# Row scatters of the first expert layer, paced differently in a one-core attention loop on Trainium2

## What is computed

```python
x = x + attn(layernorm(x))      # scores of 8 heads of width 2, leaky relu (0.2), softmax, values
x = x + ffn0(layernorm(x))      # sigmoid gates, top 6 of 64 experts, silu(x@g)*(x@u)@d, plus a shared expert
x = x + lookup(layernorm(x))    # offsets and softmax weights pick from row 0, then one projection
x = x + ffn1(layernorm(x))      # softmax gates, top 2 of 8 experts

def attn_core(q, k, v):
    scores = einsum('bmhd,bnhd->bhmn', q, k) / sqrt(dqk)
    scores = where(scores >= 0, scores, 0.2 * scores)
    return einsum('bhmn,bnhd->bmhd', softmax(scores), v)
```

## Time and profile before

| what | value |
|---|---|
| three runs | 866.82, 868.16, 869.16 us |
| median | 868.16 us |
| profiled execution: its time from the first to the last instruction (span) | 1023.1 us |
| PE busy in the profiled execution | 740.8 us, 72% |
| DVE busy | 604.7 us, 59% |
| ACT busy | 498.4 us, 49% |
| POOL busy | 425.6 us, 42% |
| mean granted TensorE clock | 0.849 of full speed |

### The profile page before, as it was taken

How to read it: one execution, slowest core, us unless ns; L and a number is a source line. 1 busy time by engine, 2 the same in 40 slices (tenths; PEclk the granted TensorE clock), 3 DMA queues, 4 the chain that set the end, 5 groups by cost and what they waited for, 6 DMA issues and landing times.

```text
span 1023.1 us, 18229 instructions
## 1 busy us (share of the span) xinstructions
PE 740.8 (72%) x6306; PEld 444.5 (43%) x6309; DVE 604.7 (59%) x1330; ACT 498.4 (49%) x747; POOL 425.6 (42%) x659
## 2 busy tenths in 40 slices
PE   5799999899889777338899960300377677599992
PEld 3322222222223222138899930200245543399992
DVE  5899998898889755446676410000265766244442
ACT  4788888778777645213444421000344432165550
POOL 4310023522442345366677667776002033345553
PEclk9999999999999878659999995655675776699997
DMA  8999999999992000528866522222000010133346
GB/s 254 249 286 288 283 273 280 288 276 291 310 358 105 19 25 31 129 87 245 258 191 171 157 54 52 54 52 51 0 11 14 19 33 32 37 37 49 48 51 138
DMA packets 83482, 142.96 MB, mean 140 GB/s; under 512 B 10736, under 2 KB 75728, under 8 KB 81888
## 3 DMA queue, kind: packets, MB, share of 16 engines
q1 hardware_dynamic: 57744, 118.07, 40.4%
q0 software_dynamic: 12784, 17.40, 7.8%
q10 hardware_dynamic: 12864, 6.33, 2.3%
HBM read 116.57 MB, written 101.34 MB: 213 GB/s over the span
## 4 chain that ended last, share of the span: by engine, by line
PE 53%; another core or an unknown queue 14%; DVE 9%; ACT 9%; issue 6%; DMA 5%; SPq 2%; POOL 1%; DVEq 0%; POOLq 0%; ACTq 0%
PE PS L664 11%; PE PS L650 8%; PE PS L1010 6%; PE PS L639 6%; DMA XP<-slots_scratch 3%; ACT PB L1146 3%; PE PS L1020 3%; PE PS L802 3%; PE PS L789 2%; PE PS L791 2%; ACT PB L1149 2%; PE PS L777 2%; PE PS L849 1%; ACT PS L1141 1%
## 5 line engine op out<-in xcount | busy, mean ns | idle before, releaser
L1679 DVE TENSOR_SCALAR PS<-PS 128x1024 f32<-128x1024 f32 x241 | 288.1, 1229 | 55.4 <-PE PS L639 30.1
L1146 ACT ACTIVATE PB<-PS 128x1024 f32<-128x1024 f32 x192 | 194.5, 1025 | 52.6 <-PE PS L650 46.0
L664 PE MATMUL PS<-PB,VS 128*32 128x256 f32 x2048 | 168.5, 402 | 3.4 <-issue 3.3
L639 PE MATMUL PS<-QS,KP 64*128 64x512 bf16 (+1 forms) x640 | 101.2, 347 | 38.1 <-ACT PB L1149 18.7
L1393 POOL DMA_INDIRECT slots_scratch<-XN,slot x96 | 93.3, 972 | 61.1 <-ACT PB L1146 36.5
L1453 POOL DMA_INDIRECT GB<-y_scratch,slotc x96 | 90.9, 946 | 37.1 <-issue 29.4
L650 PE MATMUL PS<-QM,KP 64*128 64x512 bf16 (+1 forms) x640 | 102.3, 350 | 3.5 <-DVE PS L1679 3.4
L838 PE MATMUL PS<-wshd,OH 96*128 96x128 f32 x64 | 11.7, 356 | 111.6 <-DVE OH L1820 110.7
L1463 POOL DMA_INDIRECT slots_scratch<-XN,slot x32 | 32.0, 1000 | 140.8 <-DVE slot L1964 130.8
L1483 POOL DMA_INDIRECT sums_scratch<-YO,XG x39 | 60.6, 1555 | 60.9 <-DVE YO L2034 59.7
L1149 ACT ACTIVATE PB<-PS 128x1024 f32<-128x1024 f32 x64 | 64.7, 1026 | 40.5 <-PE PS L650 26.8
(11 more groups left out here) (297 smaller groups left out, 1411.5 us busy)
## 6 DMA issues: line engine op xcount, KB each, us to landing
y_scratch<-YP SPq DMA_DIRECT2D x80, 128.0 KB, 2.5
slots_scratch<-slots_scratch SPq DMA_DIRECT2D x1, 8768.0 KB
W0GU<-in_w0gu SPq DMA_DIRECT2D x1, 6144.0 KB, 50.1
XP<-slots_scratch ACTq DMA_DIRECT2D x80, 64.0 KB, 2.8
XP<-slots_scratch SPq DMA_DIRECT2D x80, 64.0 KB, 2.7
W1GU<-in_w1gu SPq DMA_DIRECT2D x8, 512.0 KB, 4.1
W0D<-in_w0d SPq DMA_DIRECT2D x1, 3072.0 KB
XG<-slots_scratch SPq DMA_DIRECT2D x39, 68.5 KB
```

What stands on the lines that cost most here:

```text
L639: last = mm(o, keys, QS[g][r, x], start=first, stop=True, skip_group_check=not first)
L664: last = mm(PS[32 * j:32 * j + 32, at:at + HALF], VS[:, n, g * HG + j, :], PB[u // 2 % 3][:, 2 * (j % 2) + j // 2, q], start=(n == 0 and h ...
L1146: A(PB[u // 2 % 3][:, 2 * hp:2 * hp + 2, :], pair_banks(u).rearrange("p (j q) -> p j q", j=2), ACT.Exp).then_inc(sem("exp_done"), 1)
L1679: TS_(pair_banks(u), pair_banks(u), 4.0, 0.0, ALU.mult, ALU.max).then_inc(sem("relu_done"), 1)
```

## The change

The argument `pace` of `chunk_scatter` becomes a function from the scatter's number to the unit that it waits for.

- Blocks 0 and 1: scatter n waits for unit `ROUND_START[2 * s + 3] + 2 * n`, one scatter for every two units. The 24 now cover 48 units instead of 32, so the last four of each block are written among the next block's steps: two after its first `part_added`, one after its second, one after its `chunk_norm`.
- Block 2: scatters wait for units 224 + 0, 0, 2, 2, 5, 5, 7, 7, ... 27, 27: two for every 2.5 units. The cuts between the routing steps of block 3 move by one.
- Block 3: five of its twelve scatters (before: six) are written ahead of block 4's `chunk_power`, and these stand behind block 2's last pair, which waits for unit 251. Seven (before: six) come after it. Block 4 is as before.

```diff
-                    if pace is not None:
-                        pool.wait_ge(sem("exp_done"), ROUND_START[2 * s + 3] + pace * n // 3)
+                    if unit_of is not None:
+                        pool.wait_ge(sem("exp_done"), unit_of(n))
...
+                return lambda n: ROUND_START[2 * s + 3] + 2 * n
...
+                return ROUND_START[HALVES + 2] + 5 * (n // 2) // 2
...
-                for p in PARTS_OF[s]:
-                    part_added(p)
+                part_added(2 * s)
+                if s:
+                    chunk_scatter(s - 1, 20, 22, every_second_unit(s - 1))
+                part_added(2 * s + 1)
+                if s:
+                    chunk_scatter(s - 1, 22, 23, every_second_unit(s - 1))
                 chunk_norm(s)
+                if s:
+                    chunk_scatter(s - 1, 23, 24, every_second_unit(s - 1))
...
-                    chunk_scatter(s, 0, 4 * TOP0, 4)
-            chunk_scatter(2, 0, 7, None)
+                    chunk_scatter(s, 0, 20, every_second_unit(s))
+            chunk_scatter(2, 0, 6, pairs_in_last_half)
             part_added(6)
-            chunk_scatter(2, 7, 9, None)
+            chunk_scatter(2, 6, 8, pairs_in_last_half)
             chunk_norm(3)
-            chunk_scatter(2, 9, 16, None)
+            chunk_scatter(2, 8, 16, pairs_in_last_half)
             chunk_keys(3)
-            chunk_scatter(2, 16, 19, None)
+            chunk_scatter(2, 16, 20, pairs_in_last_half)
             chunk_counted(3)
-            chunk_scatter(2, 19, 24, None)
-            chunk_scatter(3, 0, 6, None)
+            chunk_scatter(2, 20, 24, pairs_in_last_half)
+            chunk_scatter(3, 0, 5)
             chunk_power(4)
-            chunk_scatter(3, 6, 2 * TOP0, None)
-            chunk_scatter(4, 0, 2 * TOP0, None)
+            chunk_scatter(3, 5, 2 * TOP0)
+            chunk_scatter(4, 0, 2 * TOP0)
```

More of the change, by code:

```diff
@@ L1382, in chunk_counted, with chunk_scatter @@
                     gp.memset(pairsum[:, 0, 0:1], 0.0).then_inc(sem("earlier_step"), 1)
-            def chunk_scatter(s, first, last, pace):
+            def chunk_scatter(s, first, last, unit_of=None):
                 c = min(s, NC - 1)
@@ L1404, in _, with every_second_unit, pairs_in_last_half @@
             pool.wait_ge(sem("x_doubled"), 3)
+            def every_second_unit(s):
+                return lambda n: ROUND_START[2 * s + 3] + 2 * n
+            def pairs_in_last_half(n):
+                return ROUND_START[HALVES + 2] + 5 * (n // 2) // 2
             for s in range(NC - 1):
-                for p in PARTS_OF[s]:
-                    part_added(p)
+                part_added(2 * s)
[4 more added lines that the diff above has]
+                    chunk_scatter(s - 1, 22, 23, every_second_unit(s - 1))
                 chunk_norm(s)
+                if s:
+                    chunk_scatter(s - 1, 23, 24, every_second_unit(s - 1))
                 chunk_keys(s)
```

## The result

The kernel after takes 870.25 us (median of 20 runs, 866.66 to 873.64), the kernel before 868.38 in 20 runs of its own (864.30 to 870.07). The ratio is 1.0028, with a 95% interval of 1.0015 to 1.0041, which is 1.3 to 3.6 us more. The forecast was 867.2, a small gain; the time rose instead, within the range and within the 0.3% that counted as the same, but on the other side and clear of no change.

A forecast was written before the change was run, and what follows sets the result against it. Scatters were taken to stall a loop full on PE and DVE, 40.8 us in the profiled execution but nearly absent from the runs. 868.2 - 1.3 (stall gain) + 0.3 (end) = 867.2 us, range 857 to 871.5.

The forecast's parts named there:

- The stall in the runs: Loop's 40.8 us of scatter losses: runs hold zero to a quarter, nearer zero; rival (0.28), at or above a quarter: 862.7, 857.
- because the gathers must keep some of their time: Reason for counting only 1.3 us of gain in the runs, from a possible 0 to 5.8.
- the 9.3 us between the table and the first expert rows: Behind the loop: up to 9.3 us counted as idle time that the runs could lack.
- POOL's issue time as a floor of ACT's wait: At the gathers: POOL needs 0.95 + 0.3 us each, 30 for the first chunk, so the 115.1 can hardly all vanish.
- -6, -17: Profiled execution's gains: 6 us from single scatters in blocks 0 and 1, 17 from pairs in the last 32 units.
- a span near 1000: Sign in the profile after: span falls by about 20 us while the runs stay within 0.3%.
- The end: Behind block 4's power: seven scatters instead of six end 0.3 us later, and twelve follow as before.
- The cover of block 4's power: Loop's end: 9.9 us covers the last pair and five scatters, 8.9, by 1.0; if lost, price about 1.0.
- POOL's steps in the last 32 units: Addition, norm and keys behind POOL's waits for pairs: cost taken as 0, bound 2.9 us.
- the third rival: Last 32 units: POOL's steps pay 2.9, the end's seven scatters 1.0, the tail 0.3; 872.4, slower; chance 0.14.
- Nothing to gain: Rival: scatters take nothing in the runs, or pacing saves nothing; 868.2 + 0.3 = 868.5; chance 0.08.
- POOL comes late: Same as the third rival: POOL's program order in the last 32 units makes it slower, 872.4; chance 0.14.

The follow-up runs named there:

- the second profile: The kernel before, unchanged, profiled again to see whether the late signals belonged to the first profiled execution; span 867.6 us, tail (last exponent's start to first expert product) 34.4.
- pairs only: Against after: blocks 0 and 1 in threes for four units as before, block 2's pairs kept, block 3's scatters six and six; 870.91 us, ratio 1.0022 to before.
- The second (-0.4 to 2.9 us): The kernel after, unchanged, timed again beside the kernel before; 870.50 us against 869.50, ratio 1.0014 (0.9995 to 1.0033).
- the other two kernels with the longer tail: Before with only five of block 3's scatters ahead of block 4's power: 870.77 us, 1.0026; block 2's pairs with block 3 six and six: 870.91, 1.0022.
- the kernel with none ahead: Against before: all twelve of block 3's scatters behind block 4's power, none ahead of it; 875.46 us against 869.50, ratio 1.0071.

## Why the prediction was wrong

**The stall in the runs.** The forecast stood on the choice to take what the runs hold of the profile's stall near zero. That was right, and still too much: 1.3 us of gain were kept "because the gathers must keep some of their time". This step failed. The first profile's loop runs from its first exponent at 46.8 to its last at 418.2, 371.4 us, against 328.7 in the second: 42.7 of the 155.5 us between the two spans. The rest goes with the wait beside the gathers (115.1 without a releaser there, none now). Neither left anything over for the runs.

Two readings had kept the 1.3 alive. One is the 9.3 us between the table and the first expert rows, which the prediction counted as idle time that the runs could lack. They are no stall: in the second profile it is 407.45 - 398.13 = 9.32 as well, and the tail is 34.4 there and 34.3 in the first. They are the rest of the train of scatters and its landing, which both profiles have. Without them the prediction's own sum leaves at most 115.1 + 40.8 - 154.9 = 1.0 of the loop's 40.8, and not 10.3. The other is POOL's issue time as a floor of ACT's wait. The gathers keep their 120 us, from the first to the last, in both profiles, and ACT's wait is gone all the same. The work behind that wait had only moved: ACT's last instruction of that line starts at 728.3 in the first profile, behind the last gather, and at 572.5 in the second, well ahead of it. From the last gather to the end it is 1023.1 - 712.8 = 310.3 us in the first profile and 867.6 - 670.8 = 196.8 in the second, 113.5 less.

Everything in the prediction that was costed from scatters in the loop (-6, -17, the test "a span near 1000") described that execution and not the kernel. The rows to see it were there: a span 154.9 above the runs' median is evidence against the execution, and the prediction used it only to scale a term that should have been struck out.

**The end.** This is the term that was mis-sized: 0.3 forecast, 1.25 measured. Its first half was good, 0.3 for the seven scatters against 0.41 in the profile. The step that failed is the half sentence "and twelve follow as before". They don't, since a train that is shifted by 0.4 us meets VectorE's operations at another point, and one scatter then takes 0.84 longer. The last scatter is on the path, as the prediction had read it from the earlier trace rows; that is why each of these shares reaches the end in full. With the gain struck out and this term at its measured size the sum is 868.16 + 1.25 = 869.4.

**The cover of block 4's power.** Forecast to hold with 1.0 to spare. Nothing was paid, but the cover was used up: in after the statistics end at 379.95 and the last of the five scatters ahead of the power at 379.99:

```profile
378.73 0.42 DVE L1675 TENSOR_TENSOR X<-X,TQ 128x256 f32<-128x256 f32 x1
378.85 1.14 POOL L1393 DMA_INDIRECT slots_scratch<-XN,slot  x1 [0.30 <-issue]
...
379.70 0.25 DVE L1634 BATCH_NORM_AGGREGATE moments<-stats 128x2 f32<-128x6 f32 x2
```

The power starts 0.10 behind the end of the statistics, as it does in before (380.51 and 380.41). The spare time went because the last pair was due while POOL still issued the pair before it, so that nine scatters ran without a gap from 368.70 to 379.99, and because the last of them took 1.14 us. With one scatter more the cover was gone, as pairs only shows, at 1.3 us.

**POOL's steps in the last 32 units.** Forecast at 0, with a bound of 2.9. Zero is right. POOL does come later than in before, as the third rival says; its addition, norm and keys (the lines of the earlier trace rows), in after and then in before's second profile:

```profile
342.74 0.73 POOL L1401 TENSOR_TENSOR X<-X,TQ 128x256 f32<-128x256 f32 x1
...
347.31 1.59 POOL L1359 TENSOR_SCALAR XN<-X,moments,rstd 128x128 f32<-128x128 f32 x2
...
359.06 0.47 POOL L1366 TENSOR_TENSOR bs<-sc,gb 128x128 f32<-128x128 f32 x1
```

```profile
341.91 0.72 POOL L1401 TENSOR_TENSOR X<-X,TQ 128x256 f32<-128x256 f32 x1
...
346.25 1.59 POOL L1359 TENSOR_SCALAR XN<-X,moments,rstd 128x128 f32<-128x128 f32 x2
...
357.14 0.46 POOL L1366 TENSOR_TENSOR bs<-sc,gb 128x128 f32<-128x128 f32 x1 [0.43 <-DVE sc L1627]
```

Counted from the start of the stretch (334.35 and 334.80) they come 1.3, 1.5 and 2.4 us later. Nobody waits for them: the stretch is 41.70 us long in both, and VectorE's idle time there is no longer. The covers that the prediction named were enough. So the measured time, on the third rival's side (872.4), came about in another way: of its three terms, 2.9 and 1.0 were not paid, and the tail's 0.3 was 1.25.

**The rivals.** The stall in the runs (0.28) is refuted by the loop's length. "Nothing to gain" (0.08) is nearest, since pacing is without effect, but it had the tail at 0.3 as well. "POOL comes late" (0.14) named the right direction and the wrong place.

**The rule that was weighed.** The prediction held the Trainium skill's page SBUF — State Buffer, section Who interferes with whom, against late starts in the trace and said that they disagree. With a second profile of the same kernel they agree: rounds with 24 scatters and with none are equal at 38.55 us. The other part of that section, named in passing and then left, bears on what decided: it says that a VectorE operation with two inputs in SBUF contends with a GpSimd instruction that reads SBUF, and that the order of issue decides which of the two is blocked. The scatter of 2.00 us, which takes its slots from SBUF and started behind the update, fits if its issue counts as such an instruction; that is a reading of this document. The other direction isn't seen here: in before's second profile the scatter of 399.40 starts 0.15 us ahead of the next update, and that update takes 1.22 us, no longer than the others. What the runs do show is that the price depends on where in VectorE's operations a scatter starts, and so on where the train stands.

**The signs named.** The granted clock of 1.00 in the last 32 units, VectorE's idle time without a releaser there (none, under the 8 named), and rounds 3 and 5 at 38.55, the low end of 38.6, lie where they were forecast. The span near 1000, the last 32 units near 55 and the gathers' unchanged 115.1 don't, all three for the first reason above. That nobody waits on POOL's norm or keys was to exclude the third rival, and does.

**What stays open.** The trace shows 1.25 us, and the first comparison gave 1.3 to 3.6, just above it. The second (-0.4 to 2.9 us) and the other two kernels with the longer tail (0.1 to 4.3, 0.2 to 3.6) hold 1.25, so a further cost isn't shown, nor excluded: from the first expert product to the end single runs differ by some 4 us (457.1 and 461.3 us in the two profiles of after), and 1 us more would be lost in that. What made the first profiled execution signal late wasn't found, and it did not come back in any of the ten later profiles.

## What to carry to other kernels

Before a stall is costed, ask whether the runs can hold it: a span far above the runs is a reason to take a second profile, not to scale the stall. A wait that both profiles show, as the 9.3 us behind the loop, is the kernel's own. Pace work for a slow issuing engine from its far end: count what must still be issued behind the last wait, since one item held back too long inside a loop that doesn't care is paid behind the loop, where nothing hides it. A train that is moved by a fraction of its spacing has another neighbour at each step, so "the rest follows as before" needs a look at what runs beside it.

## What the runs showed of the hardware

Indirect DMAs issued by POOL take 0.96 us here with 0.30 between them (the first behind one of POOL's own operations up to 1.22), and a loop that keeps PE and VectorE full doesn't notice 24 of them in 38.55 us. Such a scatter does notice VectorE's operations with two operands in SBUF. With the update moved away it took 0.96 us. Started 0.06 behind the update on 128x1024 it took 2.00 in after, and in the kernel with none ahead 1.74 if 0.32 behind, here with that kernel's rows:

```profile
396.61 1.23 DVE L1744 SCALAR_TENSOR_TENSOR keyed<-keyed,delta 128x1024 f32<-128x1024 f32 x1
396.93 1.74 POOL L1393 DMA_INDIRECT slots_scratch<-XN,slot  x1 [0.30 <-issue]
397.87 1.23 DVE L1745 TENSOR_TENSOR keyed<-keyed,chosen 128x1024 f32<-128x1024 f32 x1
```

It ends at 398.67, 0.80 behind 397.87, where VectorE's next operation starts. The same holds in after (399.89, and 399.09), and for the scatter of 1.14 us shown above, which started 0.12 behind the addition of block 4 (379.99, and 379.19, the start of the statistics). So a scatter that starts behind such an operation seems to wait until it ends, and to need 0.8 us from there, while the updates on 128x1024 keep their 1.23. The scatters of 1.48 and 1.16 us end 0.81 behind the start of an operation as well (397.55 and 396.74; 399.10 and 398.29), but they started while VectorE turned the table out of PSUM, 0.43 and 0.12 us ahead of the short operation with two operands that they also waited out. So what VectorE runs at the scatter's start doesn't explain them alone; whether the table's cast held them first isn't shown, nor is which access of the scatter is held.

And one profiled execution had a span 155.5 us longer than the second of the same kernel. Signals between engines came late in it while POOL issued indirect DMAs in the loop and beside the gathers, but not beside the train behind the loop, where the tail is 34.3 us in it and 34.4 in the second profile.
